# Order of two steps in the state-space stage of a two-layer block: dt x u on GpSimd, and B's second spread on TensorE

## The chip, the cores and the metric

The kernel is one program on one core of a Trainium2 chip. The metric is the device time of one execution in microseconds (us). The engines of the core are TensorE (PE; PEld its weight loads), VectorE (DVE), ScalarE (ACT), GpSimd (POOL) and SyncE (SP, which here issues DMAs only). Each runs its own list of instructions in order, and they meet only through semaphores.

## The reference, cut to what matters

The whole is two transformer-like layers on x of shape 8 x 512 x 128, with a Mamba block and a mixture of experts in the first, attention and a second mixture of experts in the other. The change lies in the Mamba block, which runs forward and (flipped in time) backward over every batch element:

```python
xz = u @ m_in_w.T;  xc, z = jnp.split(xz, 2, axis=-1)
xc = silu(conv(xc) + conv_b)                       # 4 taps over time
x_dbl = xc @ xproj_w.T                             # 8 columns for dt, 16 for B, 16 for C
dt = softplus(x_dbl[..., :8] @ dt_w.T + dt_b)
def step(h, inp):                                  # over time, 256 channels x 16 states
    dA = exp(dt_i[:, :, None] * A)
    h = dA * h + dt_i[:, :, None] * B_i[:, None, :] * u_i[:, :, None]
    y = einsum('bds,bs->bd', h, C_i)
y = (ys + xc * Dp) * silu(z)
return y @ m_out_w.T
```

## The kernel before, in words

`mamba_stage` handles 16 units, a unit being one batch element in one direction: 512 time steps, 256 channels, 16 states. A unit is cut into 16 steps; in each, all engines treat 128 partitions x 1024 values (2 states at once, 64 channels on each half of the partitions). For step s:

- ScalarE makes the decay, exp(dt x A), from DT, which is dt spread over the partitions (`act_da`, line 566).
- TensorE spreads B for a pair of steps into the one bank psB (`pe_spread`, line 464).
- VectorE multiplies, X = DU x psB (`dve_mult`, line 578), where DU is dt x u spread over the partitions, and scans over time, H (`dve_scan`, line 590). In the steps of `ASIDE = (3, 7, 11, 15)` there is no multiply on VectorE: GpSimd makes the product XS = DU x B from a loaded B instead (`pool_aside`, line 625).
- GpSimd multiplies the state by C, PR = H x C (`pool_state`, line 614), which from here on is called "state s".
- TensorE folds and sums PR into psY (line 484). After the last, VectorE forms YZ = psY x silu(z) (line 605), which the output matmuls "mout" read.

Meanwhile the next unit is prepared, in steps by name: convolutions c0 and c1 and gates z0 and z1, SiLU, the two halves of dt (d0, d1), exp and ln for the softplus, and xp with n1 and n2 for B and C. All these matmuls go through one bank, pp, so that each waits until ScalarE has copied the one before. GpSimd then adds the softplus's parts to dt (`pool_dt`, line 630, the array rl) and makes dt x u (`pool_du`, line 634, the array ab).

SyncE's list is `send_c`. In order, for the unit that is being prepared: wait for dt, four DMAs of DT; wait for xp's copy, store the rows of B and C; wait for dt x u, four DMAs of DU (line 655); then loads of B for the aside steps (BS) and of C (CS), each waiting for its rows and its buffer.

The order is written out by hand. A turn is a loop over j from 3 to 18, in which each engine does what belongs to that j: VectorE the scan of step j and the multiply of step j + 1; GpSimd first the aside product of step j + 2, then state j, then dt or dt x u; j of 16 to 18 are the steps 0 to 2 of the next unit. So the multiply of step 0 of the next unit comes at j = 15, ahead of scan 15, and is preceded by

```python
dve.wait_ge(du_loaded, 64 * u + 128)      # j + 1 == NS
```

H and PR have four buffers each, DU and DT two, XS and psB one. Turns 0 to 14 have a next unit (`more`); the last has none. Before the first turn each engine has its own start: TensorE does the nine steps `FIRST[:9]` of the first unit, then the first spreads of B, with c0, c1, z0, z1 of the second unit (`FIRST[9:]`, c0+ to z1+) between. `pe_spread` does something at even s only, for the pair s, s + 1.

Of the kernel before, what the change touches and what calls it, by code (L numbers as in the profile page):

```python
# [360 lines left out]
def mamba_stage(nc, W, XP, convW, diagD, negA, sel, fold, nsel, c_rows):  # L361
# [4 lines left out]
    with ExitStack() as ctx:  # L366
# [36 lines left out]
        FIRST = ("c0", "c1", "d0", "d1", "xp", "n1", "n2", "z0", "z1", "c0+", "c1+", "z0+", "z1+")  # L403
        BEFORE, EACH = len(FIRST), len(ORDER)

        def used(u, k):
            if u is None:
                return FIRST.index(k)
            if isinstance(u, int) and u == UNITS - 1:
                return BEFORE + EACH * u - 4  # L410
            return EACH * u + BEFORE + ORDER.index(k)
# [12 lines left out]
        def pe_step(pe, k, u, v, pv):  # L424

            step = k[:2] if k != "mout" and u is not None else k
            if k[-1] != "b" and (u is not None or used(u, k) >= 1):
                pe.wait_ge(pp_copied, used(u, step))
            if k == "mout":
                pe.wait_ge(fin_done, u + 1)  # L430
                for c in range(NCH):
                    last = nc.tensor.matmul(pp[:, :], w("m_out")[:, c * P:(c + 1) * P], chunk(YZ, c), start=c == 0, stop=c == NCH - 1)
            elif k[0] == "c":
                n, of = int(k[1]), v + 1 if u is not None or k.endswith("+") else v
                for tap in {"a": (0, 1), "b": (2, 3)}.get(k[-1], range(KC)):
                    last = nc.tensor.matmul(pp[:, :], convW[:, tap, n * P:(n + 1) * P], XP[:, ds((of + 1) * XW + tap, T)],  # L436
                                            start=tap == 0, stop=tap == KC - 1)
                if k.endswith("a"):
                    return
            elif k[0] == "z":  # L440
                n, of = int(k[1]), v + 1 if u is not None or k.endswith("+") else v
                last = nc.tensor.matmul(pp[:, :], w("m_in")[:, (2 + n) * P:(3 + n) * P], XP[:, ds((of + 1) * XW + PAD, T)], start=True, stop=True)
            elif k == "xp":
                for c in range(NCH):
                    last = nc.tensor.matmul(pp[0:104, :], w("xproj")[:, c * 104:(c + 1) * 104], chunk(UZ[pv], c), start=c == 0, stop=c == NCH - 1)
            elif k[0] == "n":
                rows = slice(0, 32) if k == "n1" else slice(32, 64)
                last = nc.tensor.matmul(pp[0:104, :], nsel[rows, :], ST[pv][rows, :], start=False, stop=True, skip_group_check=True)
            else:
                n = int(k[1])  # L450
                if n == 0:
                    pe.wait_ge(silu_done, v + 2 if u is not None else 1)
                for c in range(NCH):
                    last = nc.tensor.matmul(pp[:, :], dtW[:, c, n * P:(n + 1) * P], chunk(UZ[pv], c), start=c == 0, stop=c == NCH - 1)
            last.then_inc(pp_ready, 1)
# [172 lines left out]
        def pool_dt(pool, v, pv):  # L628
            pool.wait_ge(softplus_step, 2 * v + 2)
            nc.gpsimd.tensor_tensor(rl[:, :], rl[:, :], ab[:, :], ALU.add).then_inc(dtu_ready, 1)  # L630
# [5 lines left out]
        def pool_turn(pool, u, p, more):  # L636
            for j in range(3, NS + 3):
                if j + 2 in ASIDE:
                    pool_aside(pool, j + 2, u, p)
                if j + 2 - NS in ASIDE and more:  # L640
                    pool_aside(pool, j + 2 - NS, u + 1, 1 - p)
                if j < NS:
                    pool_state(pool, 16 * u + j, j, u, p)
                elif more:
                    pool_state(pool, 16 * u + j, j - NS, u + 1, 1 - p)
                if j == 7 and more:
                    pool_dt(pool, u + 1, 1 - p)
                if j == 11 and more:
                    pool_du(pool, u + 1, 1 - p)

        def spread_halves(sp, source, out, loaded):
# [32 lines left out]
        with nc.Block() as block:  # L684
            @block.sync
            def _(sp):
                send_c(sp, 0, 0, None)
                with sp.Fori(0, B - 1) as i:
                    for p in range(2):
                        send_c(sp, 2 * i + p + 1, 1 - p, 2 * i + p)  # L690
                send_c(sp, UNITS - 1, 1, UNITS - 2)

            @block.tensor
            def _(pe):
                pe.sem_inc(Y_done, 6)
                for k in FIRST[:9]:
                    pe_step(pe, k, None, 0, 0)
                for s in range(5):
                    pe_spread(pe, s, s, 0, True)
                    if s < 4:  # L700
                        pe_step(pe, FIRST[9 + s], None, 0, 0)
                with pe.Fori(0, B - 1) as i:
                    for p in range(2):
                        pe_turn(pe, 2 * i + p, p, True)
                pe_turn(pe, UNITS - 2, 0, True)
                pe_turn(pe, UNITS - 1, 1, False)
                pe.wait_ge(pp_copied, used(UNITS - 1, "mout") + 1)
                pe.wait_ge(fin_done, UNITS + 1)
                for c in range(NCH):
                    last = nc.tensor.matmul(pp[:, :], w("m_out")[:, c * P:(c + 1) * P], chunk(YZ, c), start=c == 0, stop=c == NCH - 1)  # L710
                last.then_inc(pp_ready, 1)

            @block.scalar
            def _(act):
                for k in FIRST[:9]:
                    act_step(act, k, None, 0, 0)
                    if k == "c1":
                        act_step(act, "silu_u", None, 0, 0)
                    if k == "d1":
                        act_step(act, "exp", None, 0, 0)  # L720
                        act_step(act, "ln", None, 0, 0)
                act.wait_ge(dt_loaded, 64)
                for s in range(5):
                    act_da(act, s, s, 0, True)
                    if s == 0:
                        act_step(act, "silu_z", None, 0, 0)
                    else:
                        act_step(act, FIRST[8 + s], None, 0, 0)
                with act.Fori(0, B - 1) as i:
                    for p in range(2):  # L730
                        act_turn(act, 2 * i + p, p, True)
                act_turn(act, UNITS - 2, 0, True)
                act_turn(act, UNITS - 1, 1, False)
                act.wait_ge(pp_ready, used(UNITS - 1, "mout") + 2)
                nc.scalar.copy(XP[:, UNITS * XW + PAD:UNITS * XW + PAD + T], pp[:, ::-1]).then_inc(pp_copied, 1)

            @block.vector
            def _(dve):
                nc.vector.memset(DA[:, :, :, 0], 0.0)
                nc.vector.memset(YZ[:, :], 0.0).then_inc(fin_done, 1)  # L740
                dve.sem_inc(scan_done, 2)
                dve.wait_ge(fin_done, 1)
                dve.wait_ge(du_loaded, 64)
                dve_mult(dve, 0, 0, 0, 0, True)
                for s in range(3):
                    dve_mult(dve, s + 1, (s + 1) // 2, s + 1, 0, True)
                    dve_scan(dve, s, s, 0)
                with dve.Fori(0, B - 1) as i:
                    for p in range(2):
                        dve_turn(dve, 2 * i + p, p, True)  # L750
                dve_turn(dve, UNITS - 2, 0, True)
                dve_turn(dve, UNITS - 1, 1, False)

            @block.gpsimd
            def _(pool):
                pool.sem_inc(prod_ready, 4)
                pool_dt(pool, 0, 0)
                pool_du(pool, 0, 0)
                for s in range(3):
                    if s + 2 in ASIDE:  # L760
                        pool_aside(pool, s + 2, 0, 0)
                    pool_state(pool, s, s, 0, 0)
                with pool.Fori(0, B - 1) as i:
                    for p in range(2):
                        pool_turn(pool, 2 * i + p, p, True)
                pool_turn(pool, UNITS - 2, 0, True)
                pool_turn(pool, UNITS - 1, 1, False)
# [1186 lines left out]
```

## Time and profile before

| | us |
|---|---|
| median of 3 runs | 2088.88 |
| lowest, highest | 2082.01, 2089.71 |
| the profiled execution | 2079.41 |
| its span in the trace | 2077.7 |
| mean granted TensorE clock | 0.865 of full speed |

Busy time in the span: TensorE 1640.2 us, VectorE 1349.6, ScalarE 1007.7, GpSimd 998.0. A timeline row gives the start of an instruction (or of several merged ones) in us from the start of the span, its length, the engine, the line, the operation and its tiles, and in brackets how long the engine was idle before it and what ended that. The durations of matmuls are modelled, so their ends are less sure than those of the other engines. The state-space stage lies between about 69 and 1011 us.

### The profile page before, as it was taken

The numbers are of one execution on the slowest core, as the hardware profiler recorded it, in microseconds if no ns is written. First come the engines' busy times: TensorE is split into PE (matmuls) and PEld (weight loads), VectorE is DVE, ScalarE is ACT, GpSimd is POOL, SyncE is SP. The second block draws the span as 40 slices with busy tenths as digits, with TensorE's granted clock in tenths as the row PEclk, the third lists the DMA queues.
The fourth block names the chain that finished last, engine by engine and source line by source line (L and its number), as shares of the span: only waits on it lengthen the run. The fifth ranks groups of instructions, "written<-read, shape, count | busy, mean of one in ns | idle before, by whom it ended". The sixth has DMA issues, their size and how long they took to land. (4 is left out here: it accounts for less than half of the span.)

```text
span 2077.7 us, 23347 instructions
## 1 busy us (share of the span) xinstructions
PE 1640.2 (79%) x7291; PEld 729.5 (35%) x7291; DVE 1349.6 (65%) x1529; ACT 1007.7 (48%) x1641; POOL 998.0 (48%) x524
## 2 busy tenths in 40 slices
PE   7777787777787787775855946698888889879998
PEld 5222222222222222221354734354444445543333
DVE  3089989989998999999552113466566566384444
ACT  3576666666666766674122513054444455541111
POOL 1179989989998998998442152211110110050000
PEclk8989989988988988987867976589999999978999
DMA  3134334443443333343003220502333330100001
GB/s 139 37 88 103 92 83 100 102 102 93 102 102 97 95 86 80 93 103 81 16 28 103 82 68 9 153 28 53 79 79 79 79 79 4 46 0 0 0 0 40
DMA packets 78636, 145.41 MB, mean 70 GB/s; under 512 B 10214, under 2 KB 40782, under 8 KB 76854
## 3 DMA queue, kind: packets, MB, share of 16 engines
q1 hardware_dynamic: 75350, 134.98, 25.3%
q0 software_dynamic: 3216, 9.51, 1.4%
q8 instruction: 42, 0.69, 0.1%
q14 instruction: 28, 0.23, 0.0%
HBM read 87.27 MB, written 23.53 MB: 53 GB/s over the span
## 5 line engine op out<-in xcount | busy, mean ns | idle before, releaser
L614 POOL TENSOR_TENSOR PR<-H,CS 128x1024 f32<-128x1024 f32 x256 | 599.8, 2361 | 94.1 <-DVE H L590 76.1
L590 DVE TENSOR_TENSOR_SCAN H<-DA,X 128x1024 f32<-128x1024 f32 x192 | 431.2, 2273 | 0.0
L484 PE MATMUL psY<-PR,fold 128*64 128x512 f32 x1024 | 310.3, 702 | 6.8 <-POOL PR L614 6.8
L578 DVE TENSOR_TENSOR X<-DU,psB 128x1024 f32<-128x1024 f32 x192 | 235.7, 1228 | 114.7 <-DMA DU<-ab 96.5
L1322 ACT ACTIVATE a_PT<-a_psS 128x512 f32<-128x512 f32 x320 | 181.3, 601 | 157.1 <-PE a_psS L1226 153.4
L1369 DVE TENSOR_REDUCE a_MX<-a_psM 128x1 f32<-128x384 f32 (+3 forms) x352 | 206.5, 636 | 72.9 <-PE a_psM L1241 71.7
L566 ACT ACTIVATE DA<-DT,negA 128x511 f32<-128x511 f32 x384 | 249.5, 710 | 1.1
L1240 PE MATMUL a_psM<-a_kst,a_qst 72*128 72x512 bf16 (+3 forms) x512 | 148.7, 338 | 24.6 <-DMA a_kst<-scratch_k 14.0
L1225 PE MATMUL a_psS<-a_qst,a_kst 75*128 75x512 bf16 (+3 forms) x512 | 141.6, 325 | 17.0 <-DMA a_qst<-m_scratch 15.7
L625 POOL TENSOR_TENSOR XS<-DU,BS 128x1024 f32<-128x1024 f32 x64 | 151.1, 2360 | 0.0
L464 PE MATMUL psB<-ST,sel 96*128 96x512 bf16 x128 | 56.2, 439 | 119.0 <-DVE X L578 118.4
L436 PE MATMUL pp<-work,convW 128*128 (+1 forms) x256 | 138.2, 668 | 13.6 <-ACT pre L522 11.8
L590 DVE TENSOR_TENSOR_SCAN H<-X,XS 128x1024 f32<-128x1024 f32 x64 | 146.1, 2282 | 0.0
L1437 POOL TENSOR_TENSOR work<-work 128x512 f32<-128x512 f32 x16 | 20.3, 1270 | 228.2 <-DVE work L1396 228.2
L484 PEld LDWEIGHTS psY<-PR,fold 128*64 128x64 f32 x1024 | 60.6, 151 | 195.2 <-issue 157.9
L559 ACT ACTIVATE X<-W 128x2 f32<-128x2 f32 x64 | 11.2, 175 | 203.1 <-DVE H L590 203.1
L1752 ACT ACTIVATE f_SG<-f_psG 128x512 f32<-128x512 f32 x54 | 32.2, 597 | 156.1 <-PE f_psG L1725 156.1
L1241 PE MATMUL a_psM<-a_mqk,identb 128*128 128x128 bf16 x512 | 107.5, 238 | 0.0
L1226 PE MATMUL a_psS<-a_mkq,identb 128*128 128x128 bf16 x512 | 102.9, 233 | 0.0
L1687 POOL TENSOR_TENSOR HE<-g_SG,g_UC 128x512 f32<-128x512 f32 x18 | 26.8, 1495 | 148.6 <-ACT g_UC L1616 148.4
L464 PEld LDWEIGHTS psB<-ST,sel 96*128 96x128 bf16 x128 | 12.5, 98 | 234.2 <-DVE X L578 185.5
L1255 PE MATMUL a_psO<-a_PT,a_VA 128*32 128x512 f32 (+3 forms) x1024 | 93.6, 473 | 0.8 <-ACT a_PT L1322 0.8
(268 smaller groups left out, 2739.7 us busy)
## 6 DMA issues: line engine op xcount, KB each, us to landing
CS<-c_rows SPq DMA_DIRECT2D x128, 256.0 KB, 3.9
DT<-W SPq DMA_DIRECT2D x64, 256.0 KB, 4.2
DU<-ab SPq DMA_DIRECT2D x64, 256.0 KB, 4.1
BS<-c_rows SPq DMA_DIRECT2D x64, 256.0 KB, 5.1
scratch_q<-a_partsq SPq DMA_DIRECT2D x24, 384.0 KB, 3.3
a_qst<-scratch_q SPq DMA_DIRECT2D x8, 1152.0 KB
a_kst<-scratch_k SPq DMA_DIRECT2D x24, 384.0 KB
scratch_k<-a_partsk SPq DMA_DIRECT2D x8, 384.0 KB, 4.6
```

The source lines that it names most:

```text
L436: last = nc.tensor.matmul(pp[:, :], convW[:, tap, n * P:(n + 1) * P], XP[:, ds((of + 1) * XW + tap, T)], start=tap == 0, stop=tap == KC - 1)
L484: last = nc.tensor.matmul(psY[h * HP:(h + 1) * HP, n % 2 * T:(n % 2 + 1) * T], fold[:, :], chunk(PR[n % 4], h), start=False, stop=n >= NS - 2)
L566: last = nc.scalar.activation(out[:, h, 1:T], DT[p][:, at, 1:T], ACT.Exp, scale=negA[:, at * PAIRS_S + s // 2:at * PAIRS_S + s // 2 + 1])
L578: nc.vector.tensor_tensor(both(X[s % 2][:, :]), DU[p][:, at:at + 2, :], psB[:, :].unsqueeze(1).to_broadcast([P, 2, T]), ALU.mult).then_inc ...
L590: nc.vector.tensor_tensor_scan(H[s % 4][:, :], decay, x, 0.0, ALU.mult, ALU.add).then_inc(scan_done, 1)
L614: nc.gpsimd.tensor_tensor(both(PR[s % 4][:, :]), both(H[s % 4][:, :]), CS[q % 2][:, s // 2 % 2, :].unsqueeze(1).to_broadcast([P, 2, T]), A ...
L625: nc.gpsimd.tensor_tensor(both(XS[:, :]), DU[p][:, at:at + 2, :], BS[n // 2][:, n % 2, :].unsqueeze(1).to_broadcast([P, 2, T]), ALU.mult). ...
L1225: nc.tensor.matmul(out, kst[p][:, at + i * P:at + (i + 1) * P], qst[p][:, at + i * P:at + T], start=True, stop=False)
L1240: nc.tensor.matmul(out, qst[p][0:72, at + j * P:at + (j + 1) * P], kst[p][0:72, at:at + wide], start=True, stop=False)
L1241: last = nc.tensor.matmul(out[:, j * P:wide], identb[:, :], mqk[:, :], start=False, stop=True)
L1322: nc.scalar.activation(PT[k % 4][u][:, :], psS[S_BUF[5 * k + u]][:, :], ACT.Exp, scale=DK ** -0.5).then_inc(E_done, 1)
L1369: nc.vector.tensor_reduce(MX[:, j, h0:h0 + nh], src, AX.X, ALU.max).then_inc(M_used, 1)
```

## The change

Two edits. On GpSimd, in every turn that has a next unit, dt x u is made at j = 9 and no more at j = 11: it stands behind the aside product of step 11 and state 9, and ahead of states 10 and 11. On TensorE, in the start of the stage, the second spread of B (s = 2) follows c0+ at once; c1+ comes behind it, and the third spread (s = 4) comes ahead of z1+.

```diff
@@ pool_turn
                 if j == 7 and more:
                     pool_dt(pool, u + 1, 1 - p)
-                if j == 11 and more:
+                if j == 9 and more:
                     pool_du(pool, u + 1, 1 - p)
@@ block.tensor of mamba_stage
                 for s in range(5):
                     pe_spread(pe, s, s, 0, True)
-                    if s < 4:
-                        pe_step(pe, FIRST[9 + s], None, 0, 0)
+                    if s != 1:
+                        pe_step(pe, FIRST[9 + max(0, s - 1)], None, 0, 0)
```

TensorE's order in the start, before: spread 0, c0+, c1+, spread 2, z0+, z1+, spread 4. After: spread 0, c0+, spread 2, c1+, z0+, spread 4, z1+. The orders of VectorE, ScalarE and SyncE are untouched.

## Rows read from the trace of the kernel before

**Rows 1.** The page's first part: busy us, share of the span and instructions.
```profile
PE 1640.2 (79%) x7291; PEld 729.5 (35%) x7291; DVE 1349.6 (65%) x1529; ACT 1007.7 (48%) x1641; POOL 998.0 (48%) x524
```

**Rows 2.** Waits from 60 to 1000 us: engine, line, releaser; total, times, longest.
```profile
DVE X L578 <- DMA DU<-ab: 96.5, 16, 36.4
...
POOL PR L614 <- DVE H L590: 76.1, 64, 3.4
```

**Rows 3.** Timeline of one turn, from 480 us: start, length, what, idle before and releaser.
```profile
483.58 7.00 POOL L614 TENSOR_TENSOR PR<-H,CS 128x1024 f32<-128x1024 f32 x3
...
483.71 0.33 SPq L671 DMA_DIRECT2D c_rows<-W  x1
...
490.51 2.37 POOL L634 TENSOR_TENSOR ab<-W,UZ 128x1024 f32<-128x1024 f32 x1
491.45 4.46 DVE L590 TENSOR_TENSOR_SCAN H<-DA,X 128x1024 f32<-128x1024 f32 x2
...
492.91 3.16 SPq L655 DMA_DIRECT2D DU<-ab  x4
...
495.13 2.40 POOL L625 TENSOR_TENSOR XS<-DU,BS 128x1024 f32<-128x1024 f32 x1
...
495.93 0.39 PE L464 MATMUL psB<-ST,sel 96*128 96x512 bf16 x1
...
499.93 1.23 DVE L578 TENSOR_TENSOR X<-DU,psB 128x1024 f32<-128x1024 f32 x1 [4.03 <-DMA DU<-ab]
...
501.07 2.28 DVE L590 TENSOR_TENSOR_SCAN H<-X,XS 128x1024 f32<-128x1024 f32 x1
...
518.12 2.28 DVE L590 TENSOR_TENSOR_SCAN H<-DA,X 128x1024 f32<-128x1024 f32 x1
...
520.48 2.36 POOL L614 TENSOR_TENSOR PR<-H,CS 128x1024 f32<-128x1024 f32 x1 [1.09 <-DVE H L590]
...
530.16 1.06 ACT L512 ACTIVATE ab<-ab 128x1024 f32<-128x1024 f32 x1
...
532.08 2.36 POOL L630 TENSOR_TENSOR W<-W,ab 128x1024 f32<-128x1024 f32 x1
...
550.57 2.35 POOL L625 TENSOR_TENSOR XS<-DU,BS 128x1024 f32<-128x1024 f32 x1
```

**Rows 4.** The same timeline, TensorE towards YZ.
```profile
504.67 0.39 PE L464 MATMUL psB<-ST,sel 96*128 96x512 bf16 x1 [2.71 <-DVE X L578]
...
510.85 1.08 PE L484 MATMUL psY<-PR,fold 128*64 128x512 f32 x4
```

**Rows 5.** Timeline of another turn, from 427 us, at the same place.
```profile
448.30 0.61 PE L464 MATMUL psB<-ST,sel 96*128 96x512 bf16 x1 [2.84 <-DVE X L578]
...
456.99 1.23 DVE L605 TENSOR_TENSOR YZ<-psY,UZ 128x1024 f32<-128x1024 f32 x1 [0.85 <-PE psY L484]
```

**Rows 6.** Groups of instructions from 165.58 to 945.2 us: YZ, idle before it.
```profile
L605 DVE TENSOR_TENSOR YZ<-psY,UZ 128x1024 f32<-128x1024 f32 x14 | 16.9, 1207 | 3.4 <-PE psY L484 3.4
```

**Rows 7.** Busy time by stretch: PE, PEld, DVE, ACT, POOL; clock, DMA share, GB/s.
```profile
450.00:455.00 5.00, 5.00 (x11) 1.00 (x10) 4.90 (x4) 1.60 (x4) 4.48 (x2) 0.57 0.36 105
...
505.00:510.00 5.00, 5.00 (x12) 1.09 (x11) 4.90 (x3) 0.60 (x1) 3.90 (x3) 0.66 0.42 123
```

**Rows 8.** Timeline of the start of the stage, from 55 us.
```profile
106.25 2.36 DVE L578 TENSOR_TENSOR X<-DU,psB 128x1024 f32<-128x1024 f32 x2 [36.37 <-DMA DU<-ab]
...
108.96 5.40 PE L436 MATMUL pp<-work,convW 128*128 128x512 f32 x8 [3.54 <-ACT pre L522]
...
114.67 1.23 DVE L578 TENSOR_TENSOR X<-DU,psB 128x1024 f32<-128x1024 f32 x1 [3.88 <-PE psB L464]
...
118.12 0.17 ACT L559 ACTIVATE X<-W 128x2 f32<-128x2 f32 x1 [3.04 <-DVE H L590]
...
122.72 1.23 DVE L578 TENSOR_TENSOR X<-DU,psB 128x1024 f32<-128x1024 f32 x1 [2.46 <-PE psB L464]
...
129.99 1.23 DVE L578 TENSOR_TENSOR X<-DU,psB 128x1024 f32<-128x1024 f32 x1 [0.39 <-PE psB L464]
```

## The prediction

> **What bounds the kernel now.** I read the page first. Its first part has VectorE (DVE) and GpSimd (POOL) at about equal busy shares behind TensorE [rows 1]. A share over the whole span says little, above all where two engines feed each other, so I went to the waits of the state-space stage (about 95 to 1005 us) [rows 2]: VectorE stood for DU (the spread dt x u) 16 times, 96.5 us in all. The longest, 36.4 us, is the start of the stage; the other 15, one per turn from unit to unit, make 60.1 us or 4.0 each. GpSimd waits 76.1 us for scans. Then the timeline of one turn [rows 3]. The reader should see there a line with no gap: state 9 on GpSimd at 483.58, states 10 and 11 behind it, dt x u at 490.51, the four DU transfers from 492.91, and VectorE's first multiply of the next unit at 499.93, idle 4.03 us before it. VectorE had ended scan 14 at 495.91. So per turn the path is GpSimd, then transfer, then VectorE, and only the wait at 499.93 is idle time of VectorE in the usual turn.
>
> I write S15 for the scan of step 15, XS15 for the GpSimd product that it reads, and a dash for a step of the next unit (S4').
>
> **Part 1, dt x u two steps sooner.** Nothing is added or removed: the same 22 GpSimd operations per turn in another order. The new order is XS11, state 9, dt x u, state 10, state 11, state 12, XS15, and so on.
> - *What comes sooner.* The three states from 483.58 take 7.00 us and dt x u starts at 490.51, so a slot is 2.31 us [rows 3]. dt x u moves up by two: start 483.58 + 2.31 = 485.89, end 488.26 (2.37 long). In the trace it ends at 492.88 and the multiply follows at 499.93, so 7.05 us go from its end to the use of DU. New: 488.26 + 7.05 = 495.31, sooner than scan 14's end at 495.91. The 4.03 us wait is wholly gone.
> - *Queues that it passes.* SyncE issues DT, then C's rows at 483.71, which wait for ScalarE's copy of xp, then DU [rows 3]. The copy precedes 488.26 by over 4 us, so SyncE already stands at the wait for DU and issues at once. The B and C loads behind DU follow sooner as well, save that the C load wants state 11, now done at 492.9; before the change the B loads began only after DU's issues, at 496.1 (492.91 + 3.16), so it isn't late.
> - *Its input.* dt (line 630) runs at 532.08 and its ScalarE logarithm ends at 531.22 (530.16 + 1.06) [rows 3]. Both are tied to step 7, and the step of dt isn't moved. dt x u needs only that and the SiLU, long past.
> - *What goes later.* States 10 and 11, by 2.31 us each. They are wanted by TensorE's fold matmuls and by S14 and S15, which reuse H. In the trace state 10 ends near 488.2 and state 11 near 490.6; they would end at 490.5 and 492.9, while S14 starts at 493.68 and S15 later. TensorE is in convolutions there. Cost 0; if that cover were gone, the most it could cost is 2.31 us a turn (35 us), the least 0.
> - *What is late next.* With the wait gone VectorE would do a turn in 55.44 (XS15 to XS15, 495.13 to 550.57) - 4.03 = 51.41 us. GpSimd's own work is 22 x 2.31 = 50.8. They are so near that the loop between them decides: S4' frees state 4', and from state 4' to XS15' GpSimd has 14 operations without a gap, of which dt x u is still one: 520.48 to 550.57 + 2.36 = 552.93, that is 32.45 us. XS15 releases S15, and from S15's start to S4's end VectorE takes 501.07 to 520.40 (518.12 + 2.28), 19.33 us. Each handover takes 0.08 us (520.40 to 520.48). Loop: 32.45 + 19.33 + 0.16 = 51.94. That is 0.53 above 51.41: each turn keeps 0.53 us of a new wait, for XS15. [rows 3]
> - *Margins.* DU must let the first multiply start 1.14 us before S15 (499.93 to 501.07). XS15 ends at 497.5, so it has until 496.4 and lands at 495.3: 1.1 us to spare. psB for that multiply is done at 496.3 in this turn (495.93 + 0.39), just in time. [rows 3]
> - *TensorE behind it.* YZ (line 605) waits for the last fold. From the second psB of the new unit to the last fold's end takes 7.26 us in this turn (504.67 to 511.93) [rows 4], and 8.69 to YZ at 456.99 in another, with 0.85 us of idle [rows 5]. Over 14 turns that wait is 3.4 us, four turns of 0.85 [rows 6]. Today this psB waits 2.71 us for VectorE [rows 4]; with VectorE 4 us sooner it is TensorE's own queue that sets it, about 0.8 us later than VectorE asks, against the 0.5 us of room there is. Against this, the idle stretch goes after which the granted clock is low: 0.66 in 505 to 510 and 0.57 in 450 to 455 [rows 7], between its levels of 2.4 and 1.2 GHz. Bounds: the 3.4 us vanish, or every turn pays what the slow one needs beyond the quick one, 8.69 - 7.26 = 1.4 us, 21 us in all. I take 0 change, since the two effects oppose each other.
>
> Sum: 60.1 - 15 x 0.53 = 52.1 us.
>
> The Trainium skill, "TensorE: Matmul & The Clock Gate", Part 1, says that the throttled clock is the rest state and activity releases it. By that rule removing idle time makes these matmuls quicker, and the YZ wait would vanish: 3.4 us more gained.
>
> **Does GpSimd lose by VectorE's company?** In 495.9 to 499.9 VectorE is idle. XS15, from 495.13, lies mostly there and takes 2.40 us, and dt x u, under a multiply and a scan, 2.37 [rows 3]. GpSimd isn't quicker when VectorE rests, so nothing is lost by filling the rest. The Trainium skill, "SBUF — State Buffer", section "Who interferes with whom", says the opposite: a VectorE instruction with two SBUF inputs (the scans have two) contends with a GpSimd one that reads SBUF, and the loser blocks wholly. By that rule 16 scans of 2.28 and 22 operations of 2.36 would take 88 us a turn one after the other; the turn takes 55.4, so the trace doesn't agree.
>
> **Part 2, the first unit.** The first multiplies run from 106.25 to 108.61 and free psB, but the second spread is queued behind a convolution that starts at 108.96 and, with the spread, takes 5.4 us; the third multiply stands 3.88 us until 114.67. The spread now goes ahead: psB is ready at about 109.1, before scan 0's end at about 110.8 (a scan of 2.28 us behind 108.6), and those 3.88 us go. Similarly for the next spread, ahead of the last z (2.46 us before 122.72). But the convolution itself starts no sooner, as it wants ScalarE's copy of the one before it; TensorE and ScalarE still pass four results through one bank. What comes sooner for them is ScalarE's step behind scan 1, idle 3.04 us before 118.12; about 0.2 us is lost to the spread ahead. The multiply at 129.99 waits for a spread behind the output matmuls, so it keeps only what they gain: 2 to 2.8. Bounds: 0 and 3.88 + 2.46 = 6.3; I take 2.4, from the 3.04. [rows 8]
>
> **Total.** 52.1 + 2.4 = 54.5 us. The profiled execution took 2079.4 (its span 2077.7 and 1.7 around it), so by itself 2024.9. The median of the runs is 2088.9, 9.5 above it, the runs 2082.0 to 2089.7. The gain is a difference, so I take it from the median: 2034.4, say 2034.
>
> **Rivals.**
> - *TensorE becomes the bound.* Every turn pays the 1.4 us at YZ, or the fold of a late state. Gain 52.1 - 21 + 2.4 = 33.5: 2055. For it: the four YZ waits. Against: TensorE is busy 79% of the time, a good part of it at the lower clock, and still waits for VectorE elsewhere [rows 1, 4, 7].
> - *No new wait.* XS15 proves no limit, for instance if GpSimd's 14 operations run with smaller gaps; gain 60.1 + 2.4 = 62.5: 2026. It speaks for it that the excess is only 0.53; against, that 14 durations in a row make it.
> - *The move doesn't reach VectorE.* DU's landing is held elsewhere (SyncE behind C's rows, or DU's transfers among others'). If it lands 4.6 us later than worked out, all 4.03 us stay, gain 2.4: 2086.5. Against: SyncE's row at 483.71.
> - *Slower: GpSimd, now without rest, becomes slower itself.* One mechanism: the loop above holds 14 of its operations, so the turn is 19.49 + 14 x slot. It equals today's 55.44 at a slot of 2.57 us instead of 2.32, 11% more. At 2.65 a turn takes 56.6, 1.2 longer, or 17 us over 15 turns, less 2.4: 2104. The place is state 4 to XS15. Against: the 2.40 and 2.37 us above. For it only that GpSimd has never been seen here without its rests. By the rule of the Trainium skill, "SBUF — State Buffer", cited above, this is where the time would go; the trace speaks against it, and so the chance is small.
>
> **How the numbers follow.** The forecast has 0.60, TensorE as bound 0.14, no new wait 0.11, no reach 0.08, slower 0.05, something smaller in between 0.02. The forecast's own range is 2027 to 2042 (bounds of part 2, 3.4 us, and the level of the runs). To hold 8 in 10, the range takes in the no-wait case and nearly all of TensorE's: 2022 to 2055. About 0.5%, 10 us, is what a measurement can tell from no change. Faster by more: 0.60 + 0.14 + 0.11 + 0.02 and a share of the fourth, 0.89. Within: 0.06. Slower: 0.05.
>
> **What would show it.** In the trace after: no idle before line 578 by DU in the 15 turns, dt x u directly behind state 9, S15 starting at XS15's end with some 0.5 us of idle, GpSimd's waits for scans down from 4.8 to about 1 us a turn, a turn of 51.9 to 52.2 us, and the stage's third multiply near 110.8. I am wrong if DU still releases the multiply, if YZ waits over 1 us in most turns, or if GpSimd's operations take over 2.5 us.

## The result, and the profile after

| | before | changed |
|---|---|---|
| median | 2089.30 us (4 runs) | 2030.84 us (4 runs) |
| lowest, highest | 2082.01, 2089.86 | 2020.08, 2037.29 |
| profiled span | 2077.7 | 2018.4 |

The ratio is 0.9723 with a 95% interval of 0.9672 to 0.9773: faster by 58 us, where the forecast was 54.5 us less, 2034 us. The two spans differ by 59.3 us. To see where they come from, I count VectorE's timeline from its first multiply of the stage (line 578) to the last YZ (line 605):

| us | before | changed |
|---|---|---|
| start of the span to the first multiply | 106.25 | 105.08 |
| first multiply to first YZ | 71.82 | 62.67 |
| YZ to YZ, mean of the next 14 | 55.69 | 52.35 |
| the last turn | 47.58 | 47.99 |
| first multiply to last YZ | 899.05 | 843.50 |
| last YZ to the end | 1072.4 | 1069.8 |

So 55.5 of the 59.3 us lie in the stage; the other 3.8 are where nothing was edited, within what executions of one kernel differ by (17 us between the four runs).

The waits of the changed kernel in 60 to 950 us (engine, line, releaser: total, times, longest), which answer to [rows 2]. The first line, which [rows 2] does not have, is TensorE's wait for YZ:

```profile
PE pp L432 <- DVE YZ L605: 40.9, 15, 3.6
...
DVE X L578 <- DMA DU<-ab: 36.4, 1, 36.4
...
POOL PR L614 <- DVE H L590: 20.6, 25, 1.4
...
DVE X L578 <- PE psB L464: 11.7, 19, 1.3
...
DVE YZ L605 <- PE psY L484: 5.5, 1, 5.5
DVE H L590 <- POOL XS L625: 3.4, 12, 0.4
```

The 15 waits for DU are gone; the one that is left is the start's. Two small waits have grown in their place: 19 for psB, and 12 for XS. GpSimd's waits for scans fell from 76.1 to 20.6. VectorE's wait ahead of YZ is now only that of the last unit, which was there before too (5.9 us). TensorE's wait for YZ has grown: in the 14 turns behind the first YZ it was 1.4 to 1.8 us each before and is 2.6 to 2.75 us now. One turn, in the timeline from 540 us, against [rows 3]:

```profile
563.63 2.38 POOL L634 TENSOR_TENSOR ab<-W,UZ 128x1024 f32<-128x1024 f32 x1
...
565.95 6.99 POOL L614 TENSOR_TENSOR PR<-H,CS 128x1024 f32<-128x1024 f32 x3
566.04 3.17 SPq L655 DMA_DIRECT2D DU<-ab  x4
...
571.97 0.39 PE L464 MATMUL psB<-ST,sel 96*128 96x512 bf16 x1
...
572.87 2.39 POOL L625 TENSOR_TENSOR XS<-DU,BS 128x1024 f32<-128x1024 f32 x1
...
573.79 1.23 DVE L578 TENSOR_TENSOR X<-DU,psB 128x1024 f32<-128x1024 f32 x1
...
575.18 9.33 POOL L614 TENSOR_TENSOR PR<-H,CS 128x1024 f32<-128x1024 f32 x4
575.29 2.29 DVE L590 TENSOR_TENSOR_SCAN H<-X,XS 128x1024 f32<-128x1024 f32 x1 [0.27 <-POOL XS L625]
...
586.65 1.20 DVE L605 TENSOR_TENSOR YZ<-psY,UZ 128x1024 f32<-128x1024 f32 x1
```

The reader should see dt x u ahead of the three states, DU's transfers issued 0.03 us behind its end (566.01), the multiply at 573.79 with no bracket, and scan 15 released by XS. XS15 ends at 575.26 and GpSimd goes straight on with four states: it no longer rests here.

The turns are of three kinds, in rotation: 51.87, 52.70 and 52.43 us. The longer ones hold waits for psB. Two of them, in the timelines from 526 and from 628 us:

```profile
535.46 3.42 PE L432 MATMUL pp<-YZ,W 128*128 128x512 f32 x4 [2.62 <-DVE YZ L605]
...
639.77 2.81 PE L432 MATMUL pp<-YZ,W 128*128 128x512 f32 x4 [2.72 <-DVE YZ L605]
...
642.37 2.79 PE L481 MATMUL psY<-UZ,diagD 128*128 128x512 f32 x4
...
646.69 1.23 DVE L578 TENSOR_TENSOR X<-DU,psB 128x1024 f32<-128x1024 f32 x1 [0.20 <-PE psB L464]
...
653.15 1.23 DVE L578 TENSOR_TENSOR X<-DU,psB 128x1024 f32<-128x1024 f32 x1 [0.86 <-PE psB L464]
```

In the second, TensorE has been idle for 2.72 us until YZ, and then the output matmuls take 2.81 us and the four behind them 2.79. In the turn that begins at 586.65, at a granted clock of 1.00, they take 1.98 and 1.88. Busy time by stretch (PE, PEld, DVE, ACT, POOL; then the granted clock) just behind YZ in three turns, the second of them a turn without psB waits behind YZ:

```profile
534.00:538.00 4.00, 2.54 (x3) 1.17 (x4) 4.00 (x4) 3.97 (x7) 4.00 (x3) 0.62 0.00 0
586.00:590.00 4.00, 2.10 (x5) 1.06 (x6) 4.00 (x4) 3.98 (x6) 4.00 (x3) 1.00 0.01 1
638.00:642.00 4.00, 2.23 (x4) 1.10 (x5) 4.00 (x4) 3.98 (x6) 4.00 (x3) 0.85 0.00 0
```

This holds for all 14 turns. Read from 0.8 to 5 us behind YZ, the granted clock is 1.00 in the five turns of 51.9 us and 0.59 to 0.68 in the nine longer ones. In the kernel before it is 1.00 in all 14. Yet the idle time ahead of it is 2.6 to 2.75 us in both kinds of turn, so that alone does not tell them apart.

The start of the stage, against [rows 8] (the first multiply comes 1.2 us sooner in this span):

```profile
105.08 2.36 DVE L578 TENSOR_TENSOR X<-DU,psB 128x1024 f32<-128x1024 f32 x2 [36.43 <-DMA DU<-ab]
...
109.77 1.23 DVE L578 TENSOR_TENSOR X<-DU,psB 128x1024 f32<-128x1024 f32 x1
...
115.40 1.23 DVE L578 TENSOR_TENSOR X<-DU,psB 128x1024 f32<-128x1024 f32 x1
...
117.62 1.98 PE L432 MATMUL pp<-YZ,W 128*128 128x512 f32 x4 [0.77 <-ACT pre L526]
...
122.84 1.23 DVE L578 TENSOR_TENSOR X<-DU,psB 128x1024 f32<-128x1024 f32 x1 [0.57 <-PE psB L464]
```

The two waits for the spreads of steps 2 and 4 are gone, and the multiply of step 6 comes 17.8 us behind the first one, where before it took 23.7 (129.99 - 106.25).

### The profile page after: what moved, and what is told of

The parts are those of the page before. It is cut to its first block and busy times, and to the rows that moved or that the text cites. A ratio compares the mean times of both kernels' runs of the same rounds, so it can differ in the third digit from the quotient of the medians.

```text
span 2018.4 us, 23347 instructions
## 1 busy us (share of the span) xinstructions
PE 1609.6 (80%) x7291; PEld 726.9 (36%) x7291; DVE 1350.4 (67%) x1529; ACT 1008.6 (50%) x1641; POOL 995.3 (49%) x524
## 5 line engine op out<-in xcount | busy, mean ns | idle before, releaser
L614 POOL TENSOR_TENSOR PR<-H,CS 128x1024 f32<-128x1024 f32 x256 | 598.3, 2364 | 40.5 <-DVE H L590 20.6
L484 PE MATMUL psY<-PR,fold 128*64 128x512 f32 x1024 | 295.7, 672 | 6.3 <-POOL PR L614 6.3
L464 PE MATMUL psB<-ST,sel 96*128 96x512 bf16 x128 | 54.5, 426 | 71.7 <-DVE X L578 71.1
L1240 PEld LDWEIGHTS a_psM<-a_kst,a_qst 72*128 72x128 bf16 x512 | 53.3, 105 | 91.3 <-DVE a_MX L1369 41.8
```

What stands on the lines that cost most here:

```text
L484: last = nc.tensor.matmul(psY[h * HP:(h + 1) * HP, n % 2 * T:(n % 2 + 1) * T], fold[:, :], chunk(PR[n % 4], h), start=False, stop=n >= NS - 2)
L614: nc.gpsimd.tensor_tensor(both(PR[s % 4][:, :]), both(H[s % 4][:, :]), CS[q % 2][:, s // 2 % 2, :].unsqueeze(1).to_broadcast([P, 2, T]), A ...
L1240: nc.tensor.matmul(out, qst[p][0:72, at + j * P:at + (j + 1) * P], kst[p][0:72, at:at + wide], start=True, stop=False)
```

## The experiments

Each run stood beside the kernel before on its chip, whose medians there were 2083.9 (the first four), 2084.7 (the next four) and 2069.9 (a single run, the last). The changed kernel was run again with the second four, and there it gained 48.5 us where it had gained 58.5 in the first set. Medians of one kernel in different sets thus differ by several us, so I read small differences from the turns of the traces. Each trace is one execution.

### The two parts alone

The first edit alone:

```diff
+                if j == 9 and more:      # TensorE's start as before
```

> The first edit alone: dt x u at j = 9, TensorE's start as before. Theory: the two parts add, and part 1 is worth the turns alone. In the changed kernel a turn (YZ to YZ) is 52.35 us on average against 55.69, so 15 x 3.34 = 50 us: about 2039. Turns of 51.9 to 52.7 us, first YZ near 174.7 in the span (178.07 less 3.3). Rival, by the recorded prediction's sizes: part 2 is worth only 2.4, so this one comes out 2 to 3 us above the changed kernel, about 2033.

The second alone:

```diff
+                    if s != 1:           # dt x u at j == 11 as before
+                        pe_step(pe, FIRST[9 + max(0, s - 1)], None, 0, 0)
```

> The second edit alone: B's spreads sooner in the start of the stage, dt x u at j = 11 as before. Theory: this part is worth 5 to 6 us, more than the 2.4 predicted, because TensorE runs the chain behind (z1, the output matmuls) without the idle stretch of 3 us and so at the higher clock. First YZ at 171.5 to 173.5 in the span, all later turns 55.4 to 56.4 us with 4.0 us of wait for DU each; about 2083.5. Rival: 2.4 us as predicted, first YZ at 175.5, about 2087.

| | median us | ratio to before, interval | to first YZ | mean turn | first multiply to last YZ |
|---|---|---|---|---|---|
| before | 2083.9 | | 71.82 | 55.69 | 899.05 |
| part 1 | 2032.9 | 0.9758 (0.9717 to 0.9800) | 68.30 | 52.36 | 848.82 |
| part 2 | 2080.9 | 0.9981 (0.9959 to 1.0003) | 66.08 | 55.77 | 895.16 |
| both | | | 62.67 | 52.35 | 843.50 |

The last row is from the trace above; the changed kernel was not timed on this chip. By the times, part 1 gains 51.0 us, where 50 were expected; the 2039 of the expectation was counted from 2089.3 and not from this chip's 2083.9, so that the rival's 2033 says nothing for its sizes. Part 2 gains 3.0 by the times, which lies between theory and rival and decides nothing.

In the traces the two add: up to the first YZ part 1 gives 3.5 us and part 2 gives 5.7 (66.08 against 71.82) or 5.6 (62.67 against 68.30). Part 1 gives 50.2 us over the stage. Part 2 gives 5.3 on top of part 1; alone the stage shows 3.9, since this execution had five of the turns with a YZ wait of about 0.9 us where the one before had four, and a last turn of 48.4 us in place of 47.6. Its times alone don't tell it from no change, as the interval includes 1. (Its first YZ stands at 174.9 in the span, later than expected, but its first multiply also came 2.5 us later than the one before.) The start of part 1 alone has the old waits, from 95 us:

```profile
115.99 1.23 DVE L578 TENSOR_TENSOR X<-DU,psB 128x1024 f32<-128x1024 f32 x1 [3.90 <-PE psB L464]
124.05 1.23 DVE L578 TENSOR_TENSOR X<-DU,psB 128x1024 f32<-128x1024 f32 x1 [2.46 <-PE psB L464]
131.31 1.23 DVE L578 TENSOR_TENSOR X<-DU,psB 128x1024 f32<-128x1024 f32 x1 [0.39 <-PE psB L464]
```

### Which of the two spreads

```diff
+                pe_spread(pe, 0, 0, 0, True)
+                pe_step(pe, "c0+", None, 0, 0)
+                pe_spread(pe, 2, 2, 0, True)
+                for k in FIRST[10:]:
+                    pe_step(pe, k, None, 0, 0)
+                pe_spread(pe, 4, 4, 0, True)
```

> The changed kernel with only the second spread of B moved up; the third (s = 4) is behind z1+ as before. Theory: what counts in the start is when ScalarE and TensorE get through the four results of the bank pp, and the second spread alone sets that (it lets scan 1 end sooner); the multiply of step 4 waits again some 1 to 2 us, which is made up by the step-6 wait behind it. First YZ within 0.7 us of the changed kernel's 167.75, about 2031. Rival: the two waits of the start simply add (3.9 and 2.5 us), and without the second 2.5 us are lost: first YZ at 170.2, about 2033.5.

Median 2035.5 us, 0.9746 (0.9702 to 0.9791). That is 2.6 us above part 1 alone on the same chip, within the spread of the runs of either (2026 to 2037, and 2030 to 2041), so the times do not decide here. The trace does: from the first multiply to the first YZ go 62.79 us against 62.67. The theory holds, the second spread alone gives all but 0.1 of the 5.6. (The expectation counted from the span's start; this execution reached its first multiply 4.6 us later, ahead of which the edit changes nothing, so the count from there decides.) The multiply of step 4 waits again, 1.74 us, and it costs next to nothing, since the first YZ comes no later; I take it that the path runs through the bank pp:

```profile
121.70 1.23 DVE L578 TENSOR_TENSOR X<-DU,psB 128x1024 f32<-128x1024 f32 x1 [1.74 <-PE psB L464]
```

### dt x u one step later, and one sooner

```diff
-                if j == 9 and more:
+                if j == 10 and more:
```

> The changed kernel with dt x u at j = 10 in place of 9: only one step sooner than before. Theory of the transfer: from dt x u's end to the multiply go 7.05 us; one slot later than in the changed kernel the DU of the next unit lands 2.31 us later, at 497.6 in the turn shown of before, and the multiply waits 1.7 us for it, so the turn is 55.44 - 2.31 = 53.1 us at least: about 15 x 1.0 = 15 us slower than the changed kernel, 2046, with the wait for DU back in all 15 turns (1.3 to 1.8 us each). Rival: GpSimd and TensorE already bound the turn so that one step sooner is enough: 2031 and no wait for DU.

2050.8 us, 0.9830 (0.9792 to 0.9868); the mean turn is 54.01 us, the shortest 53.10 as worked out. The expectation of 2046 took each turn as the shortest; the others hold waits for psB besides (17.5 us in all, where the changed kernel has 11.7). The wait for DU is back 15 times, 24.1 us beyond the start's (total, times, longest; then the first):

```profile
DVE X L578 <- DMA DU<-ab: 60.4, 16, 36.3
```
```profile
157.45 1.23 DVE L578 TENSOR_TENSOR X<-DU,psB 128x1024 f32<-128x1024 f32 x1 [1.62 <-DMA DU<-ab]
```

A GpSimd slot is 2.31 us, of which 1.6 show as a wait: at j = 9 DU thus lands about 0.7 us before VectorE is through with scan 14. In the turn from 540 us it is the same: 566.01 + 7.05 = 573.06, and the multiply starts at 573.79. The prediction had 0.6 us for this (495.31 against 495.91). Its 1.1 us was the margin to the later time that scan 15's wait for XS15 allows. A move by a single step gets only part of the gain.

```diff
-                if j == 9 and more:
+                if j == 8 and more:
```

> The changed kernel with dt x u at j = 8 in place of 9, directly behind state 8. Theory: at j = 9 the transfer of DU already lands about 1.1 us before it is wanted, and dt x u is still one of the 14 operations of the loop from state 4 to XS15, so nothing changes: turns 51.9, 52.7, 52.4 in rotation, mean 52.3 to 52.6, the same 0.2 to 0.4 us of wait for XS15. Rival: the transfer is still what the multiply nearly waits for and its lateness shows as psB or XS waits; then the mean turn falls by 0.3 or more.

Here both theories failed. The single run took 2045.95 us, beside a single run of the kernel before of 2069.87; one run each tells little, so the turns decide. The mean turn is 54.43 us, 2.1 longer than at j = 9. At j = 8 dt x u stands ahead of XS11 and no more behind it. Timeline from 150 us, and the waits:

```profile
199.18 2.35 POOL L634 TENSOR_TENSOR ab<-W,UZ 128x1024 f32<-128x1024 f32 x1
...
201.49 2.36 POOL L625 TENSOR_TENSOR XS<-DU,BS 128x1024 f32<-128x1024 f32 x1
...
203.88 2.29 DVE L590 TENSOR_TENSOR_SCAN H<-X,XS 128x1024 f32<-128x1024 f32 x1 [1.41 <-POOL XS L625]
```
```profile
DVE X L578 <- PE psB L464: 27.1, 34, 1.6
...
DVE H L590 <- POOL XS L625: 19.7, 15, 1.4
```

Scan 11 now waits 1.3 to 1.4 us for its XS in each of the 15 turns. I had counted one loop only, from state 4 to XS15. There is a second one, from state 4 to XS11: at j = 9 it holds 8 GpSimd operations, at j = 8 it holds 9, with VectorE's way from scan 11's start round to scan 4's end. That way is 31.9 us without the DU wait: in the turn of [rows 3] scan 11 starts at 484.47 and scan 4 ends at 520.40, less 4.03. The row of the kernel before, from the same timeline:

```profile
484.47 2.28 DVE L590 TENSOR_TENSOR_SCAN H<-X,XS 128x1024 f32<-128x1024 f32 x1
```

So the loop is 9 x 2.32 + 31.9 + 0.16 = 52.9 us, above VectorE's own 51.4; at j = 9 it is 50.6. I worked this out behind the run, but the trace bears it out: the one turn of these 14 that has no wait for psB takes 52.93 us. The others take 53.5 to 55.3 with psB waits on top. So j = 9 is not merely "soon enough": one step to either side costs 1.7 (later) or 2.1 us (sooner) a turn.

### What bounds the turn now

The changed kernel once more, beside the next three:

> The changed kernel once more, on the chip of the next three, so that they have a number beside them. The turns of the trace should be 51.87, 52.70 and 52.43 us in rotation, mean 52.35; the time 2024 to 2037.

XS15 one step sooner:

```diff
+                if j == 12:
+                    pool_aside(pool, 15, u, p)
-                if j + 2 in ASIDE:
+                if j + 2 in ASIDE and j + 2 != 15:
                     pool_aside(pool, j + 2, u, p)
```

> The changed kernel with GpSimd's XS15 made at j = 12, ahead of state 12, in place of j = 13. Theory (the loop of the prediction): the wait of scan 15 for XS15, 0.24 to 0.39 us in 12 turns, goes, since the loop from state 4 to XS15 then holds 13 GpSimd operations; TensorE's psB waits (11.7 us) stay. Turns 51.5, 52.4, 52.1, so 4 us less than the changed kernel. Rival: the three limits are tied (psB of the next unit at 0.0 to 0.1 us from VectorE's demand), another takes the wait over at once and nothing is gained: mean turn 52.3 or more.

TensorE's idle stretch filled:

```diff
             if k == "mout":
+                for _ in range(2):
+                    nc.tensor.matmul(pp[:, :], w("m_out")[:, 0:P], convW[:, 0:2, :], start=True, stop=True)
                 pe.wait_ge(fin_done, u + 1)
```

> The changed kernel with two extra matmuls (128 x 512, f32, result overwritten) on TensorE ahead of its wait for YZ in every turn, into the idle 2.6 us there. Theory (the clock): in two turns of three the granted clock is low just behind this idle stretch (0.62 at 534 to 538 in the changed kernel), the output matmuls take 2.8 to 3.4 us in place of 2.0, and the spreads for steps 6 and 8 come 0.2 to 0.86 us too late. With the stretch filled the clock stays at full and these waits go: every turn 51.9 us, psB waits under 3 us in all, 7 us faster than the changed kernel. Rival: the psB waits come from the order of TensorE's list and from ScalarE's copies, not from the clock; or the added 1.9 us delay the output matmuls: turns 52.3 or more, no gain or up to 10 us lost.

> Both of the last two together: XS15 at j = 12, two extra matmuls ahead of the wait for YZ. Theory: with both limits off, VectorE alone sets the turn, 51.4 to 51.6 us; mean 0.8 to 0.9 below the changed kernel's 52.35, so 12 us faster, 2019. Rival: the limits hide one another and the gain is that of one alone, 4 to 7 us.

| | median us | ratio to before, interval | mean turn | first multiply to last YZ | XS waits, all | psB waits, all |
|---|---|---|---|---|---|---|
| changed | 2036.2 | 0.9763 (0.9735 to 0.9790) | 52.55 | 846.47 | 3.3 | 15.0 |
| XS15 sooner | 2024.0 | 0.9700 (0.9671 to 0.9730) | 51.87 | 834.68 | 0 | 8.9 |
| stretch filled | 2023.0 | 0.9707 (0.9679 to 0.9734) | 51.91 | 838.23 | 4.0 | 4.6 |
| both | 2014.3 | 0.9664 (0.9633 to 0.9696) | 51.55 | 831.42 | 0 | 5.1 |

(The changed kernel had two turns of 53.3 and 54.0 us in this execution, with psB waits up to 1.5 us, beside the three kinds; at 52.35 the differences of the others to it are 0.2 a turn less.)

Each theory held against its rival, but not each size. With XS15 sooner the usual turn is 51.42 us, which is VectorE's own work to 0.01 (51.41 was worked out): the loop was real. Its gain is larger than expected, 0.5 to 0.7 a turn (12.2 us by the times, 4 expected), for the turns with psB waits did not stay as the theory had it, they got rarer too: 6 of 14 are longer than 51.5 us, and only 5 hold a wait for psB. XS15 sooner also shortens TensorE's wait for YZ, to 2.3 us in nine turns; just behind YZ the granted clock is 1.00 in five of these and 0.59 to 0.72 in four. With the stretch filled all 14 turns lie between 51.86 and 52.07, and the clock behind YZ is full. The psB waits came to 4.6 us, not to under 3: 3.1 of them are in the first unit, where TensorE has little to fill (0.8 us idle ahead of the output matmuls in the changed kernel) and the two matmuls make the first YZ 1.3 us later, and the other 1.5 are three waits at step 0 of a unit. Timeline and stretch of the filled kernel (lines 2 higher):

```profile
538.24 1.98 PE L431 MATMUL pp<-convW,W 128*128 128x512 f32 x4 [1.39 <-ACT pre L528]
538.34 1.20 DVE L607 TENSOR_TENSOR YZ<-psY,UZ 128x1024 f32<-128x1024 f32 x1
...
540.06 1.88 PE L434 MATMUL pp<-YZ,W 128*128 128x512 f32 x4
```
```profile
538.00:542.00 4.00, 3.76 (x9) 1.82 (x10) 4.00 (x4) 3.97 (x7) 4.00 (x3) 1.00 0.00 0
```

The output matmuls take 1.88 us, right behind the fill; it adds work to TensorE and is worth its price. The turn that stays, 51.9, is the loop's 51.94 of the prediction. The rival on the order of TensorE's list and on ScalarE's copies is out: both lists are the same but for the fill, and the waits at steps 6 and 8 went in all 14 turns. With both, 11 of 14 turns are 51.42 to 51.46. On the same chip that is 2014.3 against 2036.2 us for the changed kernel, 22 us; 15.1 of them show in the stage of the two profiled executions, the rest is in the level of the runs (2008 to 2028, and 2027 to 2041). The expectation was 12 us; by the mean turn, 51.55 against 52.35, it was met. It is the fastest version here.

## Why the prediction was right

The time, 2030.8, is 3 us from the forecast of 2034, in the forecast's own range, and by its mechanism. That it is so near says less than it seems: in another set of runs the same pair of kernels differed by 48.5 us (2084.7 and 2036.2), in this one by 58.5. The stage, 55.5 us less in one pair of traces and 52.6 with the other execution of the changed kernel, is the better measure of the 54.5. By steps:

- *The reading it starts from.* [rows 1] does not have VectorE and GpSimd at about equal busy shares: it has 65% and 48%. They are equal within the stage only, 711.1 and 715.1 of the 779.6 us from 165.6 to 945.2. Nothing in the sum rests on it.
- *dt x u lands before VectorE asks.* Right: no wait in 15 turns, and 1.6 us of it when it stands one step later. The margin to scan 14's end was put at 0.6 us and is about 0.7.
- *States 10 and 11 later, at no cost.* Right: scans 14 and 15 don't wait for them, and no wait of TensorE's folds reaches VectorE in the turns: ahead of YZ it waits in the last unit only.
- *The new wait for XS15, 0.53 us a turn.* The mechanism was right, the size half: 3.4 us in 12 turns, 0.23 on the average of 15. In the turn without psB waits behind YZ the loop's 51.94 is met (51.87). In the others the wait for XS15 is shorter, 0.24 to 0.28 us for 0.32 to 0.39. There the multiplies of steps 6 and 8 are late; I take it that GpSimd, behind state 4 in its list, catches up meanwhile, so that the two waits don't fully add.
- *TensorE behind it, 0 change at YZ.* Here the place was wrong, and a cost was missing. The YZ waits vanished (3.4 us): with the idle 2.7 us ahead of them gone, these matmuls run at a granted clock of 1.00 (2.4 GHz; 578 to 586 us of the changed kernel), where [rows 7] has 0.57 and 0.66. The Trainium skill's page "TensorE: Matmul & The Clock Gate", Part 1, says that activity releases the throttle; for these matmuls the trace agrees. But some of the idle time had only moved behind them, ahead of the output matmuls: TensorE's wait for YZ grew by about 1 us a turn, and in two turns of three those now run in part at the lower clock (1.2 GHz). The spreads for steps 6 and 8 are then late. VectorE's psB waits in the turns come to 9.9 us (11.7 less the start's 1.8), 0.66 each; 8.9 of them are at steps 6 and 8, 0.9 at step 0. The prediction had put nothing there; the spread that it had 0.8 us too late, that of step 2, is waited for in no turn, and no row shows the 0.8. The filled stretch, with a clock of 1.00 and none of the waits at steps 6 and 8 in the 14 turns, shows that this is the clock's doing.
- *Part 1 in sum.* 15 x 0.53 was subtracted, measured are 0.23 + 0.66 = 0.89 per turn above 51.41, with the 3.4 at YZ back: 60.1 - 15 x 0.89 + 3.4 = 50.2 us for 52.1, and 50.2 is what the trace of part 1 alone gives. The sum is near by luck: a cost of 9.9 us that stood nowhere was met by 3.4 at YZ and by 4.5 that the wait for XS15 fell short of.
- *Part 2, 2.4 us.* The term that was mis-sized: it gave 5.3 to 5.7, near the upper bound of 6.3. What I took as 3.0 us of ScalarE's step behind scan 1 is there, but the matmuls that follow became quicker besides: z1's takes 1.13 us for 2.08, and the output matmuls 1.98 us (117.62) for 3.78, now that TensorE no longer idles 3.8 us ahead of z1. 3.0 + 0.95 + 1.8 = 5.75. The rows of the kernel before:

```profile
120.08 2.08 PE L442 MATMUL pp<-work,W 128*128 128x512 f32 x2 [3.82 <-ACT pre L526]
...
122.92 3.78 PE L432 MATMUL pp<-YZ,W 128*128 128x512 f32 x4 [0.34 <-ACT pre L526]
```

The granted clock is 0.52 in 120 to 127 us there, and 1.00 in 115 to 120 of the changed kernel. These first output matmuls take 3.8 us in both traces with the second spread late (before, part 1 alone) and 1.98 in each without the fill that has it sooner. I had the clock in mind for part 1 and not for part 2. (The 5.4 us of [rows 8] are the convolution alone, not with the spread; that one ends at 114.58.)
- *GpSimd in VectorE's company.* Right: line 614 takes 2.364 us on average, 2.361 in the stage before, though its waits for scans fell from 76.1 to 20.6 us. The slower rival, a slot of 2.57 us, did not come about. The Trainium skill's "SBUF — State Buffer", "Who interferes with whom", says that a VectorE instruction with two SBUF inputs, as the scans have, contends with a GpSimd one that reads SBUF. No run here shows it: the scans of line 590, with GpSimd busy beside them for 97% of the time in the changed kernel (715.5 of 734.4 us from 165.6), take 2.27 us on average before and after. Page and measurement differ here, and the measurement decides.
- *The signs it named.* The turn was to take 51.9 to 52.2 us and takes 52.35 on average, by the psB waits. GpSimd's waits for scans were to fall to about 1 us a turn and fell to 1.4 (20.6 over 15). The rest came as named, the third multiply at 109.77 in a span that runs 1.2 us ahead.

The forecast was lucky twice: in the sum of part 1, as said above, and in that the errors of the two parts, -1.9 and +2.9 us, nearly cancel.

## What to carry to other kernels

Where two engines feed each other, the turn is the longest of several loops: each engine's own work, and every closed chain of handovers. Count the operations in all of them, including the products that a moved operation passes; the move by one step more lost 2 us a turn in a loop that I had not drawn. And idle time of TensorE can have a price behind it: when a wait goes, ask where TensorE will idle instead, and what it does just after.

## What the runs showed of the hardware

Two extra matmuls of 128 x 512 a turn, thrown away, made a kernel faster: 2023.0 against 2036.2 us. The granted clock behind a wait of 2.6 to 2.7 us for YZ was 0.62 and 0.85 in two turns and 1.00 in a third, with the same list of work. The rotation over three turns is in the executions of the changed kernel and of part 1 alone. The kernel before has one too: every third turn takes 56.3 us for 55.4, by the wait of 0.85 us at YZ. What spares the other turns was not tried and stays open. The stage's first multiply stood 36.3 to 40.0 us for DU in different executions of kernels whose order ahead of it is the same, and it started at 105.1 to 113.5 us of the span; why was not looked into.
